# Edge messages of a graph layer: the attribute product written by ScalarE, the gathered rows added to it by the DMA, in three tile buffers

## The chip, the cores and the metric

The kernel runs on one core of a Trainium2 chip. The core has five engines with instruction queues of their own: TensorE (PE, with weight loads shown apart as PEld), VectorE (DVE), ScalarE (ACT), GpSimd (POOL) and SyncE (SP). SP and POOL start the DMAs here. The metric is the device time of one launch in microseconds (us), lower is better; the kernel before took 2510.64 us (median of 3 runs, 2509.55 to 2512.31).

## What is computed

```python
xn = layernorm(x)                                    # (3125, 256) nodes
# graph branch: 100000 edges, sorted by dst, 3 attributes each
m   = concat([xn[src], edge_attr], axis=1)           # (100000, 259)
tmp = relu(m @ W1.T + b1)                            # the message of an edge
h_N = segment_sum(tmp, dst, num_segments=3125)
g   = relu(concat([xn, h_N], axis=1) @ W2.T);  g = g / max(norm(g), 1e-12)
# mix branch: 4 layers on xn: linear attention (8 heads), then a GELU MLP 256 -> 1024 -> 256
x = x + g + mix(xn)
# then 16 experts, 2 per node, over layernorm(x), a second layernorm, and the sum with x
```

The message is split as `relu(P[src] + attr·A)`: `P = xn @ W1[:, :256].T` is made once for the 3125 nodes and kept in HBM as `P_d`, and the product of the three attributes and the bias is a small matmul for each tile of edges. This document is about how these two summands meet.

## The kernel before, in words

**Edge tiles.** The edges are cut into 224 tiles (`NPAIR`) of 500 edges that fall into one block of 125 destination nodes. A tile lies on 125 partitions, 4 edges on each (`ST = 4`); `k` counts its two halves of 2 edges (512 columns of f32). For tile p there is:

- SP brings the attributes, `aT` (`sp_attr`, L433), two tiles deep.
- PE makes the attribute product of both halves into the two PSUM banks `edge_bank` (L366).
- POOL starts four gathers (L758), each of 125 rows of 256 f32 from `P_d` into one of the slots of `G`. `G` has 8 slots, two tiles. The gathers of tile p+2 wait for `z_done` of tile p.
- DVE adds product and gathered rows into `z` (L406). That frees the PSUM banks and the slots of `G`.
- ACT takes `zr = relu(z)`, rounded to fp32r (L374); DVE takes the rest, `zl = relu(z) - zr` (L380).
- PE multiplies `zr` and `zl` by the one-hot matrix of destinations (L358, L359: 8 matmuls) into `sum_bank`, one tile late, and DVE adds that to `agg` (L386). DVE also makes the one-hot matrix of the next tile (L393).

**Where the tiles stand.** PE, ACT and DVE have instruction orders that are written out by hand. Four tiles come ahead of the mix layers (`EG_FIRST = 2` groups of 2), 216 stand between the matmuls of the 4 mix layers (54 in each), the last four behind them. A layer has two parts. The attention part (`first`, 5 groups of nodes) has two tiles for each group, close together: on ACT they stand on both sides of five copies into `es` (L885 and L888). The second part (`second`, 5 groups) has eight tiles for each group, `step(0)` to `step(7)`: step 0 ahead of the MLP's first matmul, steps 1 to 4 behind hidden pieces f = 0, 2, 4, 6 of W1, 5 behind the queries of the next group, 6 and 7 between the five output rows of W2. ACT evicts the hidden pieces (GELU, L914) out of a ring of three PSUM banks (`RING`), and PE can't write a bank until ACT has emptied it. POOL does nothing but gathers in all that time, in tile order.

Semaphores on this path: `at_in` (attributes have landed), `e_done` (product), `g_in` (a gather has landed, one for each slot), `z_done`, `r_done` (relu), `lo_done` (zl), `s_done` (sums), `acc_done`. After the edges come the graph output, the routing and the experts, which the change doesn't touch but for a name.

Of the kernel before, what the change touches and what calls it, by code (L numbers as in the profile page):

```python
# [11 lines left out]
def build(nc, x, src, dst, edge_attr, gnn_W1, gnn_b1, gnn_W2,  # L12
# [7 lines left out]
    N, D = x.shape  # L20
# [23 lines left out]
    PG = 2  # L44
    NEG = NPAIR // PG
    PQ = NPAIR // EC
# [8 lines left out]
    assert N == T * NT and E == SE * NS and NPAIR == PG * NEG == PQ * EC and MT % 4 == 0  # L55
# [12 lines left out]
    with ExitStack() as ctx:  # L68
# [12 lines left out]
        def sem(name):  # L81
# [112 lines left out]
        ATS = [part_rows(hn, 0), part_rows(hn, 600), part_rows(TT, 0), part_rows(TT, 600), part_rows(z, 0)]  # L194
# [94 lines left out]
        st_ready, e_done, z_done, r_done, lo_done, oh_done, s_done, acc_done = (sem(n) for n in (  # L289
            "st_ready", "e_done", "z_done", "r_done", "lo_done", "oh_done", "s_done", "acc_done"))  # L290
        g_in = [sem(f"g_in{i}") for i in range(PG * ST)]
# [57 lines left out]

        def pe_sums(ge, s):  # L350
# [3 lines left out]
            for i in range(ST):  # L354
                cols = slice(D * (i % 2), D * (i % 2) + D)
                if i % 2 == 0:
                    nc.tensor.wait_ge(lo_done, ge * 2 + (i // 2 + 3))
                nc.tensor.matmul(sum_bank[0:T, 0:D], onehot[:, s, i, :], zr[:, s, i // 2, cols], start=i == 0, stop=False)  # L358
                ins = nc.tensor.matmul(sum_bank[0:T, 0:D], onehot[:, s, i, :], zl[:, i // 2, cols], start=False, stop=i == ST - 1)  # L359
# [16 lines left out]
        def dve_low(ge, s):  # L376

            for k in range(2):
                nc.vector.wait_ge(r_done, ge * 2 + (k + 1))
                nc.vector.scalar_tensor_tensor(zl[:, k, :], z[:, k, :], 0.0, zr[:, s, k, :].bitcast(f32), ALU.max, ALU.subtract).then_inc(lo_done, 1)  # L380
# [16 lines left out]
        def dve_edges(e, ge, group, s, first=False, last=False):  # L397
# [3 lines left out]
            nc.vector.wait_ge(lo_done, ge * 2 + 2)  # L401
            for k in range(2):
                nc.vector.wait_ge(e_done, ge * 2 + (k + 1))
                for j in (ST * s + 2 * k, ST * s + 2 * k + 1):
                    nc.vector.wait_ge(g_in[j], group * 16 + 16)
                nc.vector.tensor_tensor(z[:, k, :], edge_bank[k][0:ET, :],  # L406
                                        G[:, ST * s + 2 * k:ST * s + 2 * k + 2, :].rearrange("p j d -> p (j d)"),
                                        ALU.add).then_inc(z_done, 1)
            if not first:
                dve_acc(ge - 1, reg)  # L410
            dve_low(ge, s)
            if not last:
                dve_onehot(e + 1, ge + 1, 1 - s)

        def pool_edges(r):

            def group(e, ge, s):
# [4 lines left out]
                for j in range(PG * ST):  # L422
                    if j % 2 == 0:
                        v = nc.gpsimd.snap(ge * (2 * PG) + (j // 2 + 1))
                        nc.gpsimd.wait_ge(z_done, v)
# [1314 lines left out]
```

## Time and profile before

| | |
|---|---|
| median of 3 runs | 2510.64 us |
| profiled execution, its time and span | 2507.48 us, 2505.6 us |
| PE busy (matmul) | 2054.5 us, 82% |
| DVE busy | 1571.3 us, 63% |
| ACT busy | 1032.5 us, 41% |
| POOL busy | 1317.4 us, 53% |
| mean granted TensorE clock | 0.917 |

The span by stages: to about 129 us the input, `P_d` and the edge tables; 129 to 148 us the first four tiles; then the four mix layers to about 1960 us; then graph output, routing and the experts. A line of the profile names the kernel's line, engine, operation and tiles. Idle time stands behind it with what ended it. Where POOL is between two DMA issues, "issue" means that it waited for nothing the profile shows. Idle time of an engine that nobody waits for costs nothing.

### The profile page before, as it was taken

How to read it: one execution, taken by the hardware profiler on the slowest of the kernel's cores; microseconds unless marked ns; L12 is line 12 of the kernel's file. 1: busy time of each engine (PE TensorE's matmuls, PEld its weight loads, DVE VectorE, ACT ScalarE, POOL GpSimd, SP SyncE). 2: the span in 40 equal slices, each digit the busy share in tenths (PEclk: the TensorE clock that was granted, in tenths of full speed). 3: DMA queues.
4: the chain of work that ended last, by engine and by line, in shares of the span. 5: the costliest groups of instructions: out<-in, count | busy, mean ns of one | idle time of the engine just before them, and what ended most of it. 6: DMA issues, size and time to landing. Idle time of an engine off the chain costs nothing. (4 is left out here: it accounts for less than half of the span.)

```text
span 2505.6 us, 37237 instructions
## 1 busy us (share of the span) xinstructions
PE 2054.5 (82%) x10686; PEld 1654.9 (66%) x10686; DVE 1571.3 (63%) x3709; ACT 1032.5 (41%) x2338; POOL 1317.4 (53%) x1112
## 2 busy tenths in 40 slices
PE   3368899998879999987999997889999773899920
PEld 2247677776757777766777776667777563799920
DVE  4667777766767777676777767777776557111126
ACT  1234544444434444444455544455544241333310
POOL 3164666666556666755666665566666300332255
PEclk9679999999989999998999999999999786899965
DMA  8632322224222222422222233222222331899943
GB/s 199 196 70 57 74 68 66 69 69 111 58 65 66 68 68 70 119 57 67 71 69 69 68 71 102 57 71 67 68 67 71 82 84 31 294 331 329 324 124 96
DMA packets 262791, 260.81 MB, mean 104 GB/s; under 512 B 150233, under 2 KB 195158, under 8 KB 262674
## 3 DMA queue, kind: packets, MB, share of 16 engines
q0 software_dynamic: 124672, 132.82, 21.7%
q1 hardware_dynamic: 133890, 126.67, 16.5%
q10 hardware_dynamic: 4112, 0.03, 0.1%
q8 instruction: 39, 0.64, 0.1%
q14 instruction: 78, 0.64, 0.1%
HBM read 229.85 MB, written 28.39 MB: 103 GB/s over the span
## 5 line engine op out<-in xcount | busy, mean ns | idle before, releaser
L758 POOL DMA_INDIRECT G<-P_d,src_T x896 | 1152.7, 1287 | 771.2 <-DVE z L406 484.1
L374 ACT ACTIVATE zr<-z 125x512 fp32r<-125x512 f32 x448 | 274.3, 638 | 456.1 <-DVE z L406 309.8
L406 DVE TENSOR_TENSOR z<-bank,G 125x512 f32<-125x512 f32 x448 | 291.9, 686 | 231.9 <-PE bank L366 101.0
L1169 PE MATMUL bank<-TT,W_s 128*128 128x250 f32 (+1 forms) x1280 | 374.2, 444 | 5.0 <-ACT TT L827 4.2
L1040 PE MATMUL bank<-W_s,hid 128*125 128x256 f32 x1600 | 359.5, 379 | 0.0
L1040 PEld LDWEIGHTS bank<-W_s,hid 128*125 128x125 f32 x1600 | 292.6, 187 | 42.8
L1169 PEld LDWEIGHTS bank<-TT,W_s 128*128 128x128 f32 x1280 | 243.8, 197 | 110.5 <-ACT TT L827 14.2
L380 DVE SCALAR_TENSOR_TENSOR zl<-z,zr 125x512 fp32r<-125x512 f32 x448 | 288.1, 684 | 39.8 <-ACT zr L374 22.1
L358 PE MATMUL bank<-zr,onehot 125*125 125x256 f32 x896 | 270.9, 334 | 7.5 <-DVE zl L380 7.2
L1034 PE MATMUL bank<-ident,hn 125*128 125x125 f32 x700 | 136.2, 305 | 117.8 <-DVE hn L1377 50.0
L359 PE MATMUL bank<-zl,onehot 125*125 125x256 f32 x896 | 229.7, 287 | 0.0
L827 ACT ACTIVATE TT<-bank,lnc 128x125 f32<-128x125 f32 x600 | 214.3, 475 | 32.3 <-PE bank L1034 29.7
L914 ACT ACTIVATE hid<-bank,b1c 128x375 f32<-128x375 f32 x320 | 164.7, 521 | 106.1 <-PE bank L1169 90.7
L358 PEld LDWEIGHTS bank<-zr,onehot 125*125 125x125 f32 x896 | 172.9, 193 | 32.6 <-issue 12.0
L1034 PEld LDWEIGHTS bank<-ident,hn 125*128 125x128 f32 x700 | 79.5, 148 | 173.1 <-ACT TT L827 56.0
L366 PE MATMUL bank<-Wst,aT 128*125 128x512 bf16 x448 | 141.7, 397 | 54.3 <-DMA aT<-attr_d 43.0
L359 PEld LDWEIGHTS bank<-zl,onehot 125*125 125x125 f32 x896 | 173.5, 194 | 5.5
L1518 DVE TENSOR_TENSOR X<-bank,X 125x256 f32<-125x256 f32 x200 | 84.8, 424 | 121.0 <-PE bank L1040 120.7
L772 POOL DMA_INDIRECT xs<-zn_d,slot_tok x32 | 30.3, 948 | 239.0 <-DVE slot_tok L1689 164.9
L393 DVE TENSOR_TENSOR onehot<-iota_n,dst_T 125x500 fp32r<-125x500 f32 x224 | 151.6, 677 | 0.0
L1040 PE MATMUL bank<-Wv_s,TT 128*125 128x256 f32 x400 | 100.4, 390 | 29.5 <-DVE V L1445 29.5
L1040 PE MATMUL bank<-Wq_s,TT 128*125 128x256 f32 x400 | 105.1, 405 | 16.9 <-DVE qe L1472 13.1
(282 smaller groups left out, 3029.5 us busy)
## 6 DMA issues: line engine op xcount, KB each, us to landing
W_s<-in_L_ffn_w SPq DMA_DIRECT2D x64, 512.0 KB
hid<-in_L_ffn_w SPq DMA_DIRECT2D x64, 512.0 KB
G<-P_d,src_T POOLq DMA_INDIRECT x896
W_s<-in_L_mix_W SPq DMA_DIRECT2D x8, 1024.0 KB
aT<-attr_d SPq DMA_DIRECT2D x224, 31.2 KB
slot_out<-yo SPq DMA_DIRECT2D x32, 128.0 KB
slot_out<-eT SPq DMA_DIRECT2D x32, 128.0 KB
attr_d<-hn SPq DMA_DIRECT2D x12, 246.1 KB, 4.0
```

The source lines that it names most:

```text
L358: nc.tensor.matmul(sum_bank[0:T, 0:D], onehot[:, s, i, :], zr[:, s, i // 2, cols], start=i == 0, stop=False)
L359: ins = nc.tensor.matmul(sum_bank[0:T, 0:D], onehot[:, s, i, :], zl[:, i // 2, cols], start=False, stop=i == ST - 1)
L374: nc.scalar.activation(zr[:, s, k, :], z[:, k, :], ACT.Relu).then_inc(r_done, 1)
L380: nc.vector.scalar_tensor_tensor(zl[:, k, :], z[:, k, :], 0.0, zr[:, s, k, :].bitcast(f32), ALU.max, ALU.subtract).then_inc(lo_done, 1)
L393: nc.vector.tensor_tensor(onehot[:, s, :, :], iota_n[0:ET, :].unsqueeze(1).to_broadcast([ET, ST, T]), dst_T[:, ds(e * ST, ST)].unsqueeze(2 ...
L406: nc.vector.tensor_tensor(z[:, k, :], edge_bank[k][0:ET, :], G[:, ST * s + 2 * k:ST * s + 2 * k + 2, :].rearrange("p j d -> p (j d)"), ALU ...
L758: pool.indirect_dma_start(G[:, j, :], None, P_d[:, :], bass.IndirectOffsetOnAxis(ap=src_T[:, at:at + 1], axis=0)).then_inc(g_in[j], 16)
L827: ins = act.activation(TT[:, k, tt_cols(j)], RING[loc % 3][:, 128 * k:128 * k + T], ACT.Identity, bias=shift(k), scale=gain(k))
L914: act.activation(hid[:, f, a * T:b * T], RING[loc % 3][:, 0:(b - a) * T], ACT.Gelu, bias=b1c[:, f:f + 1]).then_inc(ring_act, 1)
L1034: ins = pe.transpose(to[:, 128 * k:128 * k + parts], rows[:, 128 * k:128 * k + 128], ident[0:parts, 0:parts])
L1040: ins = pe.matmul(to[0:parts, 0:cols], a, b, start=i == 0, stop=i == len(products) - 1)
L1169: ins = pe.matmul(to[:, 0:(b - a) * T], W1_s[:, k, part], TT[:, k, TT_PIECES[pc]], start=k == 0, stop=k == KD - 1)
```

## The change

It does the following, and nothing outside of the edges changes but line numbers and the name of one scratch area (`z` becomes `G` in `ATS`):

- The sum z by DVE and the tile `z` are gone. ACT copies the product out of `edge_bank` into the tile's slots of `G` (`act_attr`), and the gathers are issued with `compute_op=ALU.add`: they add the rows of `P_d` to what stands in `G`.
- `G` has 12 slots, three tiles (`GS = 3`). `zl` has two buffers.
- ACT reads `G` for relu (`act_relu`) and waits there for `g_in`; behind it stands the copy for the tile after next. DVE's `dve_low` reads `G`.
- PE's product for tile p+2 stands where that of tile p stood.
- A gather of tile p+2 waits for `v_done`, the copy of the product of tile p+2.

```diff
+    GS = 3
-        G = sb("G", [ET, PG * ST, D])
-        z = sb("z", [ET, 2, 2 * D])
-        zl = sb("zl", [ET, 2, 2 * D], f32r)
+        G = sb("G", [ET, GS * ST, D])
+        zl = sb("zl", [ET, PG, 2, 2 * D], f32r)
+        def pe_products(ge, group, s):
+            nc.tensor.wait_ge(at_in[s], group * 16 + 16)
+            for k in range(2):
+                nc.tensor.wait_ge(v_done, ge * 2 + (k + 1))
+                nc.tensor.matmul(edge_bank[k][0:ET, :], aT[:, s, :], Wst[:, 2 * k * D:2 * (k + 1) * D],
+                                 start=True, stop=True).then_inc(e_done, 1)
...
-        def pe_edges(ge, group, s, first=False):
-            nc.tensor.wait_ge(at_in[s], group * 16 + 16)
-            for k in range(2):
-                nc.tensor.wait_ge(z_done, ge * 2 + (k + 3))
-                nc.tensor.matmul(edge_bank[k][0:ET, :], aT[:, s, :], Wst[:, 2 * k * D:2 * (k + 1) * D],
-                                 start=True, stop=True).then_inc(e_done, 1)
+        def pe_edges(ge, group, s, first=False, last=False):
+
+            if not last:
+                pe_products(ge + PG, group + 1, s)
             if not first:
                 pe_sums(ge - 1, 1 - s)
-        def act_edges(ge, s):
+        def act_attr(ge, q, gap=GS):
             for k in range(2):
-                nc.scalar.wait_ge(z_done, ge * 2 + (k + 5))
-                nc.scalar.activation(zr[:, s, k, :], z[:, k, :], ACT.Relu).then_inc(r_done, 1)
+                nc.scalar.wait_ge(e_done, ge * 2 + (k + 1))
+                nc.scalar.wait_ge(lo_done, ge * 2 + (k + 1 + 2 * (GS - gap)))
+                nc.scalar.activation(messages(q, k), edge_bank[k][0:ET, :], ACT.Copy).then_inc(v_done, 1)
+
+        def act_relu(ge, q, s, arrived):
+            nc.scalar.wait_ge(s_done, ge + 1)
+            for k in range(2):
+                for j in (ST * q + 2 * k, ST * q + 2 * k + 1):
+                    nc.scalar.wait_ge(g_in[j], arrived * 16)
+                nc.scalar.activation(zr[:, s, k, :], messages(q, k), ACT.Relu).then_inc(r_done, 1)
...
-        def dve_edges(e, ge, group, s, first=False, last=False):
+        def dve_edges(e, ge, q, s, first=False, last=False):
             reg = None if first else block_of(e - 1)
             if first:
                 dve_onehot(e, ge, s)
-            nc.vector.wait_ge(lo_done, ge * 2 + 2)
-            for k in range(2):
-                nc.vector.wait_ge(e_done, ge * 2 + (k + 1))
-                for j in (ST * s + 2 * k, ST * s + 2 * k + 1):
-                    nc.vector.wait_ge(g_in[j], group * 16 + 16)
-                nc.vector.tensor_tensor(z[:, k, :], edge_bank[k][0:ET, :],
-                                        G[:, ST * s + 2 * k:ST * s + 2 * k + 2, :].rearrange("p j d -> p (j d)"),
-                                        ALU.add).then_inc(z_done, 1)
+            dve_low(ge, q, s)
             if not first:
                 dve_acc(ge - 1, reg)
-            dve_low(ge, s)
             if not last:
                 dve_onehot(e + 1, ge + 1, 1 - s)
+
+        def pool_gather(at, q, i):
+            nc.gpsimd.indirect_dma_start(G[:, ST * q + i, :], None, P_d[:, :],
+                                         bass.IndirectOffsetOnAxis(ap=at, axis=0), compute_op=ALU.add).then_inc(g_in[ST * q + i], 16)
...
-                    if j % 2 == 0:
-                        pool.wait_ge(z_done, e * (2 * PG) + j // 2 + 1)
...
+            for p in range(NPAIR):
+                for i in range(ST):
+                    if i % 2 == 0:
+                        pool.wait_ge(v_done, p * 2 + (i // 2 + 3))
+                    pool_gather(src_T[:, p * ST + i:p * ST + i + 1], p % GS, i)
...
+                act_relu(p, p % GS, s, p // GS + 1)
+                if p + PG < NPAIR:
+                    act_attr(p + PG, (p + PG) % GS)
```

How the instructions stand now. On ACT, in the attention part, around the copies into `es` (they empty PE's transposes of `eT`), before:

```order
L374 ACTIVATE zr<-z 125x512 [waits z_done] x2
L833 ACTIVATE es<-bank 125x256 [waits ring_full] x5
L374 ACTIVATE zr<-z 125x512 [waits z_done] x2
L880 ACTIVATE corr<-cdiff 128x2 [waits cd_done]
L882 ACTIVATE eT<-bank,nb 128x375 x2
```

and now:

```order
L392 ACTIVATE zr<-G 125x512 [waits g_in9,g_in8,s_done]
L392 ACTIVATE zr<-G 125x512 [waits g_in11,g_in10]
L385 ACTIVATE G<-bank 125x512 [waits lo_done,e_done] x2
L843 ACTIVATE es<-bank 125x256 [waits ring_full] x5
L392 ACTIVATE zr<-G 125x512 [waits g_in1,g_in0,s_done]
L392 ACTIVATE zr<-G 125x512 [waits g_in3,g_in2]
L385 ACTIVATE G<-bank 125x512 [waits lo_done,e_done] x2
L895 ACTIVATE corr<-cdiff 128x2 [waits cd_done]
```

Two copies have come between the two relus, and each pair of relus waits for DMAs (`g_in`) where it waited for DVE.

On ACT, in the second part of a layer, around the hidden pieces of the MLP (`hid` is evicted out of the ring that PE writes), before:

```order
L914 ACTIVATE hid<-bank,b1c 128x375 [waits ring_full]
L914 ACTIVATE hid<-bank,b1c 128x250 [waits ring_full]
L374 ACTIVATE zr<-z 125x512 [waits z_done] x2
L914 ACTIVATE hid<-bank,b1c 128x375 [waits ring_full]
L914 ACTIVATE hid<-bank,b1c 128x250 [waits ring_full]
```

and now:

```order
L929 ACTIVATE hid<-bank,b1c 128x375 [waits ring_full]
L929 ACTIVATE hid<-bank,b1c 128x250 [waits ring_full]
L392 ACTIVATE zr<-G 125x512 [waits g_in5,g_in4,s_done]
L392 ACTIVATE zr<-G 125x512 [waits g_in7,g_in6]
L385 ACTIVATE G<-bank 125x512 [waits lo_done,e_done] x2
L929 ACTIVATE hid<-bank,b1c 128x375 [waits ring_full]
L929 ACTIVATE hid<-bank,b1c 128x250 [waits ring_full]
```

The evictions of `hid` now stand behind the landing of gathered rows and behind two copies.

## Rows read from the trace of the kernel before

**Rows 1.** Busy time of a stretch of layers, counts in brackets, clock, DMA share.
```profile
core 0: us, PE busy (x) PEld busy (x) DVE busy (x) ACT busy (x) POOL busy (x), PEclk, DMA share, GB/s
770.00:1170.00 400.00, 364.78 (x1856) 289.88 (x1856) 288.48 (x662) 187.29 (x400) 246.98 (x192) 0.98 0.30 73
```

**Rows 2.** PE's waits in 405 to 1950 us: total us, times, longest.
```profile
PE bank L1040 <- DVE V L1445: 21.8, 15, 3.2
PE bank L1034 <- DVE hn L1525: 20.5, 18, 1.2
PE bank L1034 <- DVE hn L1377: 14.1, 3, 4.8
PE bank L1107 <- ACT es L833: 12.4, 15, 0.8
PE bank L1040 <- DVE qe L1472: 10.3, 5, 3.4
PE bank L1034 <- DVE qe L1480: 8.5, 3, 2.8
...
PE bank L358 <- DVE zl L380: 3.4, 6, 0.8
```

**Rows 3.** The page's costliest groups: busy, mean ns, idle before, what ended it.
```profile
L758 POOL DMA_INDIRECT G<-P_d,src_T x896 | 1152.7, 1287 | 771.2 <-DVE z L406 484.1
L374 ACT ACTIVATE zr<-z 125x512 fp32r<-125x512 f32 x448 | 274.3, 638 | 456.1 <-DVE z L406 309.8
L406 DVE TENSOR_TENSOR z<-bank,G 125x512 f32<-125x512 f32 x448 | 291.9, 686 | 231.9 <-PE bank L366 101.0
```

**Rows 4.** POOL in order of time, 806 to 856 us: start, us, idle before.
```profile
809.28 1.21 POOL L758 DMA_INDIRECT G<-P_d,src_T  x1 [11.63 <-DVE z L406]
...
826.51 1.35 POOL L758 DMA_INDIRECT G<-P_d,src_T  x1 [0.31 <-issue]
...
839.02 1.21 POOL L758 DMA_INDIRECT G<-P_d,src_T  x1 [0.31 <-issue]
```

**Rows 5.** DVE in order of time, same stretch: first and fifth tile's sums.
```profile
808.31 1.28 DVE L406 TENSOR_TENSOR z<-bank,G 125x512 f32<-125x512 f32 x2
...
830.87 0.69 DVE L406 TENSOR_TENSOR z<-bank,G 125x512 f32<-125x512 f32 x1 [0.66 <-DMA G<-P_d,src_T]
```

**Rows 6.** ACT in order of time, one group of the second part.
```profile
811.04 1.19 ACT L374 ACTIVATE zr<-z 125x512 fp32r<-125x512 f32 x2
...
819.41 1.23 ACT L374 ACTIVATE zr<-z 125x512 fp32r<-125x512 f32 x2 [0.85 <-DVE z L406]
...
822.82 0.57 ACT L914 ACTIVATE hid<-bank,b1c 128x375 f32<-128x375 f32 x1 [0.79 <-issue]
...
824.66 1.23 ACT L374 ACTIVATE zr<-z 125x512 fp32r<-125x512 f32 x2 [0.52 <-issue]
...
830.24 0.63 ACT L374 ACTIVATE zr<-z 125x512 fp32r<-125x512 f32 x1 [0.53 <-DVE z L406]
...
842.22 1.23 ACT L374 ACTIVATE zr<-z 125x512 fp32r<-125x512 f32 x2 [5.52 <-DVE z L406]
...
874.78 1.20 ACT L374 ACTIVATE zr<-z 125x512 fp32r<-125x512 f32 x2
```

**Rows 7.** POOL and DVE in order of time, around the first four tiles.
```profile
88.99 1.24 POOL L758 DMA_INDIRECT G<-P_d,src_T  x1 [42.83 <-issue]
...
129.18 1.29 DVE L406 TENSOR_TENSOR z<-bank,G 125x512 f32<-125x512 f32 x2 [15.45 <-PE bank L366]
...
145.87 0.69 DVE L406 TENSOR_TENSOR z<-bank,G 125x512 f32<-125x512 f32 x1 [2.83 <-DMA G<-P_d,src_T]
```

**Rows 8.** ACT in order of time, two tiles of the attention part.
```profile
1098.41 1.19 ACT L374 ACTIVATE zr<-z 125x512 fp32r<-125x512 f32 x2
1099.44 1.66 ACT L833 ACTIVATE es<-bank 125x256 f32<-125x256 f32 x5
1101.72 1.23 ACT L374 ACTIVATE zr<-z 125x512 fp32r<-125x512 f32 x2 [0.61 <-DVE z L406]
```

**Rows 9.** Two lines of indirect DMAs on POOL: ns min/median/max, first and last start.
```profile
L758 POOL DMA_INDIRECT G<-P_d,src_T x768: 1205/1211/2137, 379.2 to 1968.8; - x192
...
L772 POOL DMA_INDIRECT xs<-zn_d,slot_tok x32: 944/944/969, 2134.9 to 2365.1; - x32
```

More of the change, by code:

```diff
@@ L54, in build @@
     MT = (2 * N + NE * (SL - 1)) // SL
[L55 removed]
+    assert N == T * NT and E == SE * NS and NPAIR == PG * NEG == PQ * EC and MT % 4 == 0 and NPAIR % GS == PG
     def dram(name, shape, dt):
@@ L287, in build @@
         a_out = [sem(f"a_out{i}") for i in range(AB)]
[L289 to L291 removed]
+        st_ready, e_done, v_done, r_done, lo_done, oh_done, s_done, acc_done = (sem(n) for n in (
+            "st_ready", "e_done", "v_done", "r_done", "lo_done", "oh_done", "s_done", "acc_done"))
+        g_in = [sem(f"g_in{i}") for i in range(GS * ST)]
         at_in = [sem(f"at_in{i}") for i in range(PG)]
@@ L629, in layer @@
                     weights_A(l + 1)
-                with sp.Fori(EG_B + 1, EG_L + 1) as g:
+                with sp.Fori(EG_B + 2, EG_L + (1 if last else 2)) as g:
                     e = l * EG_L + g + EG_FIRST
@@ L854, in both @@
                     edges(group, s)
+            for p in range(PG):
+                act_attr(p, p)
             for e in range(EG_FIRST):
@@ L929, in _, with again, act_first @@
                 both(e)
-            more_rounds(act, act_tables, lambda r: both(r * NEG), lambda e, ge: both(ge), lambda r: both(r * NEG + (NEG - 1)))
+            def again(ge, last=False):
+                for s in range(PG):
+                    act_relu(ge * PG + s, s, s, ge + GATHERS)
+                    if not last:
+                        act_attr(ge * PG + (s + PG), s, gap=PG)
+            def act_first(r):
+                for s in range(PG):
+                    act_attr(r * NPAIR + s, s, gap=PG)
+                again(r * NEG)
+            more_rounds(act, act_tables, act_first, lambda e, ge: again(ge), lambda r: again(r * NEG + (NEG - 1), last=True))
             def rows_T(u):
@@ L1061, in _, with edges, both @@
             pe.wait_ge(t_cp, 5)
-            def edges(group, s, first=False):
-                pe_edges(group * PG + s, group, s, first=first)
-            def both(group, first=False):
+            def edges(group, s, first=False, last=False):
+                pe_edges(group * PG + s, group, s, first=first, last=last)
+            def both(group, first=False, last=False):
+                if first:
+                    for s in range(PG):
+                        pe_products(group * PG + s, group, s)
                 for s in range(PG):
-                    edges(group, s, first=first and s == 0)
+                    edges(group, s, first=first and s == 0, last=last)
             for e in range(EG_FIRST):
@@ L1185, in _ @@
                 second(NG - 1, last=True)
-            with pe.Fori(EG_LAST, NEG) as e:
-                both(e)
+            for e in range(EG_LAST, NEG):
+                both(e, last=e == NEG - 1)
             pe_sums(NPAIR - 1, 1)
@@ L1195, in pe_last @@
             def pe_last(r):
-                both(r * NEG + (NEG - 1))
+                both(r * NEG + (NEG - 1), last=True)
                 pe_sums(r * NPAIR + (NPAIR - 1), 1)
@@ L1395, in edges @@
             def edges(e, group, s, first=False, last=False):
-                dve_edges(e * PG + s, group * PG + s, group, s, first=first, last=last)
+                dve_edges(e * PG + s, group * PG + s, (e * PG + s) % GS if isinstance(group, int) else s, s, first=first, last=last)
             def both(e, group, first=False, last=False):
```

38 lines of the change are left out of this document (17 added, 21 removed).

## The prediction

> **What bounds the kernel now.** I read the busy time by stages first, then who waits for whom, then the order of time on POOL, DVE and ACT over one group of nodes. In the mix layers PE is busy 364.78 of 400 us at a clock of 0.98 [rows 1]. So the layers, where 216 of the 224 tiles stand, are PE's, and DVE (288), POOL (247) and ACT (187) have room on average. PE's idle time there that DVE ends is 21.8 + 20.5 + 14.1 + 10.3 + 8.5 + 3.4 = 78.6 us [rows 2]; that bounds what a relieved DVE can give back. POOL has the least obvious schedule. It idles 771 us, but 484 of that waits for the sum z [rows 3], and then it works in bursts: from 809.28 us it issues 20 gathers without a pause, the last at 839.02 [rows 4], so (839.02 + 1.21 + 0.30 - 809.28) / 5 = 6.25 us for a tile of four. PE's steps in that stretch are closer: relus start at 819.41 and 824.66 [rows 6]. The burst is survived by a head start. Its last tile but one is just caught: the gather that starts at 826.51 is issued until 827.86, and z runs at 830.87, released by that DMA [rows 4, 5]. From the end of an issue to the landing it is therefore 3.0 us.
>
> **What the change removes.** DVE loses 448 sums of 686 ns, 292 us busy [rows 3]. Most of it is cover that PE never waited for. The waits in front of L1445 and L1525 end on work that stands ahead of the tile steps or in a chain of its own, so of the 78.6 us I take 10, with 0 and 78.6 as the ends.
>
> **What it adds on ACT.** 448 copies of 125x512. The nearest row is the relu of the same size, 638 ns, two in 1.23 us [rows 3, 6]; the end above is 0.75 us each, and nothing below 0.6 is to be expected from the same 512 columns. It is 286 us more on an engine at 187 of 400. In the MLP they cost nothing by themselves: behind two hidden pieces ACT has an idle 0.79 us before one eviction [rows 6] and the wait in front of relu, and PE's ring of three banks covers the order. In the attention part they are exposed. There PE waits for the copies into `es` [rows 2], and the second relu follows the first by 1101.72 - 1098.41 = 3.31 us, of which relu and copies take 2.7 [rows 8]. With two attribute copies between them it is 1.23 + 1.23 + 1.66 + about 0.1 = 4.2 us, 0.9 more, 20 groups: **+18 us**.
>
> **What it moves: the start of the gathers.** Three buffers sound like a deeper queue. They are not: the copy for tile p+2 stands behind relu of tile p on ACT, and only then may POOL start on p+2. Two tiles are outstanding, as before, and the third buffer only holds the tile that is being read. Worse, the start moves from DVE's sum to ACT's step.
>
> - MLP bursts. POOL's burst starts at 809.28, after z at 808.31 [rows 4, 5]. ACT's step 0 comes behind ten evictions at 811.04 [rows 6]; two relus (1.23) and the first copy (0.64) put the burst's start at 812.9, 3.6 us later. At 6.25 us for a tile and 3.0 us to land (issue gap of 0.3 not counted), the second halves of the next tiles are there at 821.9, 828.1 and 834.4. The relus of these halves start at 820.0 (819.41 + 0.6), 825.3 and 830.9 [rows 6]. The lateness is 1.9, 2.8 and 3.5 us. The fourth, 840.6, is in time for 842.22 + 0.6. While ACT waits for rows, the evictions behind it wait, and PE runs out of banks after 0.8 us of slack. So 3.5 - 0.8 = 2.7 us in each group, 20 groups: **+54 us**. The period of a group, 874.78 - 811.04 = 63.7 us, becomes that much longer.
> - Tail of a group (steps 5 to 7) and end of a layer. PE's product at step p waited for z(p-1); it now waits for the copy for tile p+1, which stands behind relu(p-1), the same landing and 1.23 us more. 20 groups: **+25 us**.
> - First four tiles. POOL fetches two tiles at 88.99, long before the first z at 129.18, and the fourth tile's last sum runs at 145.87 [rows 7]. In the changed kernel no gather can start before the first product has been copied, about 130 us. Sixteen gathers in series take 25 us, landing 3: the last relu comes at 158 us for 146.6 now: **+11 us**.
>
> Sum with gathers that cost what they cost now: 18 + 54 + 25 + 11 - 10 = +98 us.
>
> **What the accumulating gather costs.** No row shows one. It does all that a plain gather does and reads the destination besides, so it is not cheaper. The ends: 1.21 us as now, and 2.13, the longest gather [rows 9]; landing between 3.0 us and twice that, 6.0. The row nearest in kind is the pair of rows 9: the same instruction with nearly as many rows of the same size takes 944 ns into one place and 1211 ns into another, so the layout of its descriptors is worth 0.27 us. An addition must fetch the destination too. I take half of that step, 1.35 us, and 1 us more to land. A tile then costs POOL 6.8 us for 6.25. At the third tile of a burst that is 3 x 0.55 + 1.0 = 2.6 us later, 20 groups, 53 us. In the tail the landing alone counts, 1.0 x 20 = 20 us. The start gets 16 x 0.14 + 1 = 3 us. Together **+76 us**.
>
> Two pages of the Trainium skill speak against this change. "DMA: Bandwidth & Descriptors" (Rules for kernel authors) says that an accumulating DMA reads its destination before it writes it, and "Collectives: The Full Stack" (The bandwidth ceiling) that a DMA that adds runs at half the rate since it needs two reads, not because the addition costs anything. The first page (Why a DMA increments its semaphore by 16) also says that the number of engines is the largest divisor up to 16 of the slowest dimension: 5 for 125 rows. At its 27 GiB/s for an engine, 25 rows of 1 KB are an estimated 0.9 us, so a second read would put the landing at 3.9 us. The trace shows only the 3.0 us as a whole; by that estimate the sum stays where it is, by a rate that isn't changed it would be 20 to 40 us less.
>
> **Sum.** The profiled execution takes 2507.5 us (span 2505.6), 3 below the median of the runs, 2510.6. 2507.5 + 98 + 76 = 2681.5; I forecast **2680 us**. A measurement of this kernel tells 0.2%, 5 us, from no change.
>
> **Rivals.**
>
> 1. *The addition is free on POOL and in the transfer.* The first sum stands alone: 2507.5 + 98 = 2605 us. For it: POOL's median doesn't move with anything in 768 gathers [rows 9]. Against: a second read of each row. Chance 0.26.
> 2. *POOL becomes the bound of the layers.* Eight tiles must be issued in a group's 63.7 us, that is 1.99 us for a gather with its gap of 0.31. From 1.68 us on, POOL sets the period outright, and from 1.55 on it is late at the end of a group as well. At 1.8 us: 8 x 4 x 2.11 = 67.5 us plus the start and the landing that nothing covers (about 5 us), 9 us more in each of 20 groups, 180, beside 18 + 11 + 25 and the pairs of the attention part (4 x 0.6 us in 20 groups, 48): about 2790 us. At the upper end of 2.13 us it is near 2900. For it: POOL is already the engine with the longest unbroken work. Against: the step from 1.21 is large. Chance 0.20.
> 3. *Faster: DVE's relief is worth more than the lateness.* DVE is the engine that ends most of PE's idle time [rows 2]. If the relu waits under 0.8 us at the third tile of a burst, so that the ring hides it, only 18 + 11 remain against up to 78.6: at best 2507.5 + 29 - 78.6 = 2458 us, and with half of the relief 2497. The lateness of 3.5 us would have to be wrong by 2.7, for instance by ACT's step 0 coming two microseconds earlier. Chance 0.07.
> 4. *No difference.* Lateness and relief cancel, within 5 us of 2510. Chance 0.04.
>
> **How the numbers follow.** The forecast has 0.43 and its own range 2630 to 2750; rivals 1 to 4 have 0.26, 0.20, 0.07 and 0.04. Slower by over 0.2% has 0.89, no change 0.04, faster 0.07. For the range I leave out faster and same (0.11) and the upper half of rival 2, and take rival 1 with 25 us below it: 2580 to 2860.
>
> **What would show it.** The gather's line on POOL with its median: 1.21 for rival 1, 1.3 to 1.5 for the forecast, 1.7 or more for rival 2. ACT's relu should wait for `DMA G` in total for some hundreds of us, where DVE waited; PE's idle time in the second part should stand ahead of W1 products and be ended by ACT; POOL's idle time should shrink from 771 us; the first relu pair of a burst should be in time and the third late. The first four tiles should end some 11 to 15 us later. I am wrong if relu hardly waits for DMAs, or if POOL's burst starts earlier than ACT's step 0 lets it.

## The result and the profile after

The changed kernel takes 2902.62 us (median of 4 runs, 2901.37 to 2903.93), the kernel before 2511.47 us (median of 4, 2509.55 to 2512.36) on the same chip: ratio 1.156, 95% interval 1.154 to 1.158. It is 391 us slower, where I forecast 170 slower and gave a range that ended at 2860. The direction held and the size did not; what happened is nearest to rival 2, POOL as the bound of the layers' second part.

The first view is the page's list of costliest groups of the changed kernel (busy us, mean ns of one, idle us before, what ended it), which answers to [rows 3]:

```profile
L427 POOL DMA_INDIRECT G<-P_d,src_T x896 | 1827.4, 2039 | 489.8 <-issue 248.9
L399 DVE SCALAR_TENSOR_TENSOR zl<-G,zr 125x512 fp32r<-125x512 f32 x448 | 303.2, 693 | 935.2 <-ACT zr L392 911.6
L392 ACT ACTIVATE zr<-G 125x512 fp32r<-125x512 f32 x448 | 277.7, 641 | 740.2 <-DMA G<-P_d,src_T 739.5
L1198 PE MATMUL bank<-TT,W_s 128*128 128x250 f32 (+1 forms) x1280 | 412.7, 471 | 127.5 <-ACT hid L929 120.9
...
L385 ACT ACTIVATE G<-bank 125x512 f32<-125x512 f32 x448 | 242.2, 598 | 44.9 <-issue 36.1
```

The gather's mean went from 1287 to 2039 ns, 675 us more on POOL. The relu now waits 739.5 us for gathers, and DVE sits idle behind relu. The copy itself is cheap, 598 ns. POOL's idle time is 489.8 us, of which 248.9 is only the gap between two issues (`issue`). The view of POOL's operations on `G` gives the median, to be set beside [rows 9] (ns as minimum/median/maximum), and then what POOL's idle time ended on (us, times):

```profile
L427 POOL DMA_INDIRECT G<-P_d,src_T x896: 1986/1992/2849, 124.6 to 2361.1; - x180
...
  ACT G L385: 241.0, 82
```

The median is 1992 ns where it was 1211. Of the 771 us that POOL had to spare, 241 are left as real waits, in 82 pieces. In order of time, POOL around one MLP group (start, us, idle before), which answers to [rows 4]:

```profile
952.11 1.99 POOL L427 DMA_INDIRECT G<-P_d,src_T  x1 [5.31 <-ACT G L385]
954.41 1.99 POOL L427 DMA_INDIRECT G<-P_d,src_T  x1 [0.31 <-issue]
...
1025.14 1.99 POOL L427 DMA_INDIRECT G<-P_d,src_T  x1 [0.31 <-issue]
1030.85 2.01 POOL L427 DMA_INDIRECT G<-P_d,src_T  x1 [3.71 <-ACT G L385]
```

Between 952.11 and 1027.13 stand 32 gathers without a pause, all eight tiles of a group; before, the burst was 20 gathers long. A group lasts 1030.85 - 952.11 = 78.7 us. Of that, 75.0 are POOL's own time (32 x 2.30 = 73.6 at the median, and four gathers that took 2.4 to 2.5 us), and 3.7 us are a wait for the next copy. Most groups took 63.7 to 66.4 us before. Over all 20 groups POOL waits for 97 us of 1561 in pauses of over 0.4 us; in the kernel before it was 233 of 1245. ACT in order of time in the same group, beside [rows 6]:

```profile
950.13 1.20 ACT L392 ACTIVATE zr<-G 125x512 fp32r<-125x512 f32 x2
951.17 1.13 ACT L385 ACTIVATE G<-bank 125x512 f32<-125x512 f32 x2
...
960.74 0.63 ACT L392 ACTIVATE zr<-G 125x512 fp32r<-125x512 f32 x1 [1.79 <-DMA G<-P_d,src_T]
965.27 0.63 ACT L392 ACTIVATE zr<-G 125x512 fp32r<-125x512 f32 x1 [3.90 <-DMA G<-P_d,src_T]
...
975.11 0.63 ACT L392 ACTIVATE zr<-G 125x512 fp32r<-125x512 f32 x1 [4.65 <-DMA G<-P_d,src_T]
...
983.54 0.63 ACT L392 ACTIVATE zr<-G 125x512 fp32r<-125x512 f32 x1 [4.05 <-DMA G<-P_d,src_T]
```

The relus come two and two no longer, and the second half of each tile waits about 4 us for its rows. The gather that starts at 954.41 is issued until 956.40 and its relu runs at 960.74: 4.3 us to the waiting engine, where [rows 4, 5] had 3.0. Over all relus that a gather released, the median from the end of the issue is 4.4 us; over the sums z of the kernel before it is 3.1. Who pays is in the list of PE's waits from 400 to 2300 us (total us, times, longest), beside [rows 2]:

```profile
PE bank L1198 <- ACT hid L929: 115.4, 38, 4.8
PE bank L1060 <- ACT hid L929: 54.2, 15, 5.0
```

PE waits for the evictions that stand behind a waiting relu, as the prediction said; before, no such row was in the list. A stretch of 400 us in the same layer, which begins three tiles later than that of [rows 1]:

```profile
945.00:1345.00 400.00, 329.33 (x1514) 253.05 (x1515) 191.42 (x455) 194.18 (x420) 327.71 (x161) 0.91 0.48 63
```

POOL has gone from 247 to 328 busy of 400; with a gap of 0.31 us behind each of 161 gathers that is 378, nearly full. PE does 1514 matmuls where it did 1856. The share of DMA time is 0.48 where it was 0.30, at fewer GB/s. The page's row of POOL's DMA queue (packets, MB, share of 16 engines) has what goes with it, first of before, then of after:

```profile
q0 software_dynamic: 124672, 132.82, 21.7%
```

```profile
q0 software_dynamic: 382720, 133.81, 36.1%
```

Nearly the same bytes go in three times as many packets: 258048 more, 288 for each of 896 gathers.

### The profile page after: what moved, and what is told of

Same layout as the page of the kernel before. It is cut to its first block and busy times, and to the rows that moved or that the text cites. A ratio compares the mean times of both kernels' runs of the same rounds, so it can differ in the third digit from the quotient of the medians.

```text
span 2901.7 us, 37993 instructions
## 1 busy us (share of the span) xinstructions
PE 2170.2 (75%) x10686; PEld 1720.6 (59%) x10686; DVE 1320.1 (45%) x3261; ACT 1227.8 (42%) x2786; POOL 1992.1 (69%) x1112
## 3 DMA queue, kind: packets, MB, share of 16 engines
q0 software_dynamic: 382720, 133.81, 36.1%
## 5 line engine op out<-in xcount | busy, mean ns | idle before, releaser
L427 POOL DMA_INDIRECT G<-P_d,src_T x896 | 1827.4, 2039 | 489.8 <-issue 248.9
L399 DVE SCALAR_TENSOR_TENSOR zl<-G,zr 125x512 fp32r<-125x512 f32 x448 | 303.2, 693 | 935.2 <-ACT zr L392 911.6
L392 ACT ACTIVATE zr<-G 125x512 fp32r<-125x512 f32 x448 | 277.7, 641 | 740.2 <-DMA G<-P_d,src_T 739.5
L1198 PE MATMUL bank<-TT,W_s 128*128 128x250 f32 (+1 forms) x1280 | 412.7, 471 | 127.5 <-ACT hid L929 120.9
L366 PE MATMUL bank<-zr,onehot 125*125 125x256 f32 x896 | 293.6, 355 | 17.9 <-DVE agg L405 15.4
L385 ACT ACTIVATE G<-bank 125x512 f32<-125x512 f32 x448 | 242.2, 598 | 44.9 <-issue 36.1
L367 PE MATMUL bank<-zl,onehot 125*125 125x256 f32 x896 | 247.7, 303 | 0.0
L1060 PEld LDWEIGHTS bank<-ident,hn 125*128 125x128 f32 x700 | 82.0, 153 | 240.0 <-ACT hid L929 63.7
L366 PEld LDWEIGHTS bank<-zr,onehot 125*125 125x125 f32 x896 | 189.3, 211 | 44.1 <-issue 30.2
L355 PEld LDWEIGHTS bank<-Wst,aT 128*125 128x125 bf16 x448 | 64.7, 150 | 151.2 <-issue 82.5
L1066 PE MATMUL bank<-Wq_s,TT 128*125 128x256 f32 x400 | 125.8, 472 | 31.1 <-DVE qe L1501 29.2
L1066 PEld LDWEIGHTS bank<-Wq_s,TT 128*125 128x125 f32 x400 | 90.9, 242 | 61.4 <-DVE qe L1501 43.2
```

The source lines that it names most:

```text
L385: nc.scalar.activation(messages(q, k), edge_bank[k][0:ET, :], ACT.Copy).then_inc(v_done, 1)
L392: nc.scalar.activation(zr[:, s, k, :], messages(q, k), ACT.Relu).then_inc(r_done, 1)
L399: nc.vector.scalar_tensor_tensor(zl[:, s, k, :], messages(q, k), 0.0, zr[:, s, k, :].bitcast(f32), ALU.max, ALU.subtract).then_inc(lo_done, 1)
L427: nc.gpsimd.indirect_dma_start(G[:, ST * q + i, :], None, P_d[:, :], bass.IndirectOffsetOnAxis(ap=at, axis=0), compute_op=ALU.add).then_in ...
L1060: ins = pe.transpose(to[:, 128 * k:128 * k + parts], rows[:, 128 * k:128 * k + 128], ident[0:parts, 0:parts])
L1066: ins = pe.matmul(to[0:parts, 0:cols], a, b, start=i == 0, stop=i == len(products) - 1)
```

## Experiments

Three theories were to be told apart: that POOL's time for an adding gather makes the loss, on top of a smaller one from the order of work (theory T), that the order of work makes it (S), and that the DMA traffic makes it (D). The table has the time of three parts of the edge work, read from the starts of the relus in ACT's order of time: from the launch to the relu of the fourth tile, the first 14 tiles of each of the four layers (attention part), their other 40 tiles (MLP part, 20 groups), and what is left of the span. "Tile" is POOL's time for four gathers with all that stands between them, at the median. A time in the table is of the profiled execution, a ratio of the runs on one chip; "plain" is a gather without the addition (in the changed kernel the rows of `P_d` then overwrite the attribute product), "filler" a memset on POOL of that many us behind each gather.

| kernel | ratio (95%) | tile | start | attention | MLP | rest |
|---|---|---|---|---|---|---|
| before | 1 | 6.1 | 143.1 | 558.0 | 1245.0 | 559.5 |
| after | 1.156 (1.154 to 1.158) | 9.2 | 161.2 | 598.4 | 1561.1 | 581.0 |
| before, adding | 1.129 (1.125 to 1.133) | 9.2 | 159.6 | 593.5 | 1497.0 | 575.4 |
| after, plain | 1.032 (1.028 to 1.035) | 6.1 | 148.6 | 558.3 | 1311.3 | 571.2 |
| after, copy first | 1.149 (1.145 to 1.152) | 9.2 | 159.3 | 618.4 | 1528.0 | 583.3 |
| after, plain, copy first | 1.021 (1.020 to 1.023) | 6.1 | 149.8 | 567.3 | 1277.7 | 562.5 |
| after, 128 rows | 1.075 (1.071 to 1.078) | 7.4 | 152.2 | 576.6 | 1389.3 | 572.1 |
| after, plain, filler 0.80 | 1.144 (1.142 to 1.147) | 8.8 | 157.2 | 648.8 | 1491.9 | 579.8 |
| after, plain, filler 0.42 | 1.082 (1.080 to 1.083) | 7.3 | 153.1 | 594.7 | 1389.8 | 568.5 |
| after, plain, copy first, 128 rows | 1.003 (1.002 to 1.005) | 5.0 | 145.1 | 551.5 | 1261.4 | 555.4 |
| before, 128 rows | 0.990 (0.989 to 0.992) | 5.0 | 137.6 | 540.7 | 1242.0 | 555.5 |
| before, three deep | 0.996 (0.994 to 0.997) | 6.1 | 142.0 | 554.0 | 1241.0 | 554.1 |
| before, three deep, 128 rows | 0.988 (0.987 to 0.990) | 5.0 | 136.9 | 541.5 | 1242.0 | 553.8 |

### The change cut in two: the order without the addition, the addition without the order

```diff
 # after, plain: the gather of the changed kernel
-bass.IndirectOffsetOnAxis(ap=at, axis=0), compute_op=ALU.add)
+bass.IndirectOffsetOnAxis(ap=at, axis=0))
 # before, adding: the gather of the kernel before, and G cleared once
-bass.IndirectOffsetOnAxis(ap=src_T[:, at:at + 1], axis=0))
+bass.IndirectOffsetOnAxis(ap=src_T[:, at:at + 1], axis=0), compute_op=ALU.add)
```

> The changed kernel with plain gathers (no addition): the rows of P_d overwrite the attribute product, so the product is left out of the messages; order, waits and buffers stay. Theory T (the 391 us are POOL's time for an adding gather, 1.99 us for 1.21, on top of a schedule that costs about 100 us by itself): the gather is back at 1.21 us, landing 3.0 to 3.2 us, the kernel takes 2600 to 2625 us, a group of the second part 66 to 67 us. Theory S (the schedule costs most of it: ACT's evictions behind the rows, copies ahead of them): above 2750 us although the gather takes 1.21 us. Theory D (the additional DMA traffic slows the others): 2510 to 2540 us, since the traffic is gone.

> The kernel before with adding gathers and nothing else: G is cleared once and each gather adds to what stands there, so the message is wrong by the older rows in G; DVE still makes z. Theory T: the gather takes 1.99 us with a gap of 0.3 and lands after 4.0 us; eight tiles need 73.6 us where a group takes 63.7, so the second part follows POOL: 2760 to 2820 us. Theory S: the order is that of before, with DVE in front of ACT, so no more than 2560 us. Theory D: in between, with longer plain DMAs (weights, attributes) in the trace.

The order alone takes 2590.67 us (2585.78 to 2594.38), the addition alone 2832.71 (2827.81 to 2837.38), for 2512.45 of the kernel before. That is +78 and +320; the sum, 398, is the whole loss of 391 within the runs' spread. So the addition's cost is there without any of ScalarE's copies or the third buffer, which rules out theory S for most of the loss. The order alone came out 9 us below the range that I gave for it, though a full group takes 67 to 69 us where I expected 66 to 67. The gather of each, first the order alone (ns minimum/median/maximum):

```profile
L427 POOL DMA_INDIRECT G<-P_d,src_T x896: 1206/1214/2457, 124.4 to 2050.0; - x180
```

```profile
L759 POOL DMA_INDIRECT G<-P_d,src_T x896: 1982/1992/3055, 89.7 to 2287.5; - x180
```

The median follows the addition, and neither the order nor the third buffer. With the addition alone, the page's group of DVE's sum shows the wait that relu has in the changed kernel (columns as above):

```profile
L406 DVE TENSOR_TENSOR z<-bank,G 125x512 f32<-125x512 f32 x448 | 301.2, 688 | 590.7 <-DMA G<-P_d,src_T 471.1
```

The 320 us are above what I expected of it. Its MLP groups last 75.2 to 76.7 us (the last of each layer is shorter), and POOL pauses for no more than 1.5 us in any of them, where the changed kernel's pauses come to some 5. So in this kernel POOL's own time is the period of a group.

### ScalarE's copy ahead of the relu

```diff
-                act_relu(p, p % GS, s, p // GS + 1)
                 if p + PG < NPAIR:
                     act_attr(p + PG, (p + PG) % GS)
+                act_relu(p, p % GS, s, p // GS + 1)
```

> The changed kernel with ACT's copy for tile p+2 ahead of relu of tile p: the gathers start about 1.2 us earlier after each step and no longer behind the landing of tile p. Theory T: POOL is the bound of the second part and doesn't care for the order: 2885 to 2903 us, gather 1.99 us. Theory S: the order is what hurts, so at least 100 us come back: 2800 us or less.

> The changed kernel without the addition in the gathers (the attribute product is lost from G, so its output isn't the reference's), and with ScalarE's copies for tile p+2 placed ahead of the relu of tile p instead of behind it. It is compared with the same kernel with the copies behind the relu (2590.7 us), 78 us over the kernel before. If those 78 us are the late start of the bursts (two relus of 1.23 us ahead of the first copy, in the MLP groups and at the tails), the copies ahead give back up to 1.2 us in each of 20 groups at the third tile and as much in the tail: 2590 - 20 to 45 = 2545 to 2570 us. If the 78 us are ScalarE's added 286 us of copies themselves, wherever they stand, the time stays at 2590 within 6 us. If the pair in the attention part counts, its gap (3.57 us) shrinks toward 3.3.

With the addition 2884.3 us (2881.99 to 2890.88), 18 less than the changed kernel; without it 2559.07 us (2557.75 to 2564.98), beside 2507.24 of the kernel before on the same chip. The ratio falls from 1.032 to 1.021, some 27 us. All of it is in the MLP part (1311.3 to 1277.7) and the rest; the attention part gets 9 us longer. So about a third of the order's 78 us comes from the copy's place behind the relu; that it does so by the late start of the bursts fits the MLP part and isn't shown separately. With the addition the MLP part gains as much (1561.1 to 1528.0), but the attention part gives 20 of it back.

### Gathers of 128 rows in the changed kernel

```diff
-        src_T = sb("src_T", [ET, NPAIR * ST], i32)
+        src_T = sb("src_T", [128, NPAIR * ST], i32)
-        G = sb("G", [ET, GS * ST, D])
+        G = sb("G", [128, GS * ST, D])
```

> The changed kernel with gathers of 128 rows for 125 (G and the indices have 128 partitions, the last three rows aren't read). It asks what the 1.99 us consist of. If POOL's time goes by the rows that one DMA engine gets (the plain gather took 1.21 us with 125 rows, 0.94 with 128), the addition adds little: gather 1.15 to 1.3 us, landing 3.3 to 3.8 us, kernel 2600 to 2660 us. If POOL pays 0.78 us for about 125 additions whatever their place: gather 1.7 us, kernel 2790 to 2840 us. If nothing changes (1.99 us): 2900 us.

2696.66 us (2691.93 to 2699.97): three more rows in each gather make the kernel 206 us faster. The gather, and the queue:

```profile
L427 POOL DMA_INDIRECT G<-P_d,src_T x896: 1532/1541/2727, 123.7 to 2153.7; - x180
...
q0 software_dynamic: 139008, 134.59, 34.2%
```

The median falls between the two that I had named, 1.2 and 1.7. The packets fall from 382720 to 139008, but the share of DMA time stays at 34.2% (36.1 with 125 rows). Of a shorter span that is 12% less DMA time, 920 us for 1048, so this run alone doesn't clear the traffic; the filler of the next section does, with plain transfers. Packets of this queue and POOL's median have the same order in the four kinds, but no common price: plain 128 rows 52992 and 946 ns, plain 125 rows 124672 and 1211, adding 128 rows 139008 and 1541, adding 125 rows 382720 and 1992. Between the second and the third, 14336 packets more go with 330 ns more; between the third and the fourth, 243712 with 451. What in the addition holds POOL stays open.

### A filler on POOL in place of the addition

```diff
                     pool_gather(src_T[:, p * ST + i:p * ST + i + 1], p % GS, i)
+                    pool.wait_ge(padded, p * ST + i)
+                    pool.memset(pad[:, :], 0.0).then_inc(padded, 1)
```

`pad` has 820 columns of bf16 in the one kernel and 360 in the other; the gathers are plain.

> The changed kernel without the addition (the attribute product is lost from G, so its output isn't the reference's), with a memset of a scratch tile of some 0.8 us on POOL behind each of the 896 gathers. POOL's time for a gather with what follows it is then about that of the adding gather (1.99 + 0.31 us), while the transfer and its landing stay plain (2.8 us). If POOL's occupation is what the addition costs, the group of eight tiles comes to 8 x 4 x 2.3 = 74 us plus 3 to 5, and the time to 2820 to 2880 us, within 30 to 70 us of the changed kernel's 2902; the rest is the landing (1.1 us more, once a group and at each pair of the attention part). If the transfer is what costs (the reads of the destination, the single packets of a row, the later landing), the filler lies mostly beside it and the time stays under 2700 us.

> The same with half the filler, some 0.4 us behind each gather, so that gather, gap and filler make about 1.9 us. Eight tiles then take POOL 61 us, less than the 68 to 69 us that a group takes without a filler, but the bursts are later by 1.6 us a tile. If the group's period is the larger of POOL's sum and the schedule's with the burst's lateness on top (a knee), the time is 2650 to 2720 us, clearly less than half way from 2591 to the run with the full filler in slope only if the burst's lateness is small. If every us of POOL's time counts from the start (a straight line), half of the full filler's loss: 2700 to 2735 us. If POOL has room, 2591 to 2630 us.

2874.72 us (2867.27 to 2879.49) with the long filler, 2714.12 (2707.84 to 2715.57) with the short one. POOL in order of time with the long one:

```profile
901.45 1.22 POOL L429 DMA_INDIRECT G<-P_d,src_T  x1 [0.18 <-issue]
902.68 0.80 POOL L775 MEMSET pad<- 125x820 bf16 x1
903.66 1.22 POOL L429 DMA_INDIRECT G<-P_d,src_T  x1 [0.18 <-issue]
```

A plain gather and a memset take 2.21 us where the adding gather takes 2.30 with its gap, and the time is within 28 us of the changed kernel's with no addition anywhere: 284 of the 312 us between "after, plain" and "after" are back. The queue has the plain 124672 packets and 19.0% of DMA time, so theory D is ruled out for most of the loss. The page shows the same wait, though the transfers are the plain ones:

```profile
L394 ACT ACTIVATE zr<-G 125x512 fp32r<-125x512 f32 x448 | 274.7, 637 | 633.7 <-DMA G<-P_d,src_T 626.0
```

The three fillers, none, short and long, also give the shape of the curve. POOL's step is 1.52, 1.82 and 2.21 us at 2590.7, 2714.1 and 2874.7 us: 896 x 0.30 = 269 us more on POOL cost 123, and 896 x 0.39 = 349 more cost 161, both 0.46 us for each us. In the MLP part alone it is 0.41 for both. The ranges that I had given for a knee and for a straight line overlap at 2714 us, so it is the equal slopes that speak for a line. My knee stood at a gather of 1.55 to 1.68 us, which is a step of 1.86 to 1.99, between the two fillers; the fillers show none. The adding gathers bend a little: their steps of 1.52 (plain), 1.85 (128 rows) and 2.30 us have MLP parts of 1311.3, 1389.3 and 1561.1 us, 0.37 and then 0.59 us for each us of POOL. With a step of 1.82 a group lasts 71.6 us, 13 more than POOL's 58.2. With the long filler that distance has closed to 5.7 (76.4 for 70.7), near the 5.1 of the changed kernel (78.7 for 73.6). One pair needs no rate: the short filler and the adding gathers of 128 rows have nearly the same step, 1.82 and 1.85, and the same MLP part, 1389.8 and 1389.3 us, the one without and the other with the addition.

The filler isn't neutral. The long one is 50 us slower than the changed kernel in the attention part (648.8 for 598.4). DVE's own work is longer beside the memsets, in both parts: against "after, plain" its busy time grows by 55 us in the attention part and by 55 in the MLP part. As one example, the groups of one line that writes `hn` (times, total us, mean ns), 500 to 1800 us of "after, plain" and 500 to 2000 us of the long filler:

```profile
L1406 DVE TENSOR_SCALAR hn<-X,mvA,rstd_t 125x256 f32<-125x256 f32 x145 | 59.8, 476 | 0.0
```

```profile
L1410 DVE TENSOR_SCALAR hn<-X,mvA,rstd_t 125x256 f32<-125x256 f32 x140 | 103.1, 799 | 0.0
```

So the whole's 284 of 312 us says too much: part of it is DVE's slower work. PE's waits for `V`, made in the attention part, are 17.8 us in all with no filler, 65.5 with the long one and 30.2 in the changed kernel; its waits for `hn`, which grow in the MLP part above all, are 73, 100 and 85. The MLP part is the better comparison, though not a clean one. The addition costs 249.8 us there (1311.3 to 1561.1) and the filler 180.6. Its step is 0.09 us shorter than the adding gather's, which over 640 gathers is 58 us of POOL's time: 24 us at the rate of 0.41 that the fillers show, 58 if POOL is full. As an estimate, the time that POOL is held then accounts for 205 to 239 of 250 us. The rest, 11 to 45, is left for the later landing and all else, and up to some 28 us of the filler's own share may be DVE's.

### What the order is worth when POOL is relieved

This is the changed kernel without the addition, with the copy first and 128 rows.

> The changed kernel without the addition (same part left out), with the copy for tile p+2 ahead of the relu of tile p and with gathers of 128 rows: everything in the change's order that its loss on POOL and at the start of the bursts can be relieved of. Its DVE is still without the sum z. If the rest of the schedule's loss (52 us after the copies were moved) is waiting for gathers, a tile of 4 x 1.25 us on POOL takes most of it away: 2505 to 2525 us, and DVE's relief could show, below the old order with the same gathers (2481 us) only if it is worth more than all that is left. If the rest is ScalarE's own work in front of PE's evictions, 2545 to 2560 us.

2515.51 us (2513.87 to 2521.83), ratio 1.003, 0.3% slower than the kernel before and 1.3% slower than the old order with the same gathers. Here relu hardly waits for gathers any more (18.8 us in all), and ACT waits in front of its copies instead (page's groups):

```profile
L392 ACT ACTIVATE zr<-G 125x512 fp32r<-125x512 f32 x448 | 262.0, 648 | 18.8 <-DMA G<-P_d,src_T 18.8
...
L385 ACT ACTIVATE G<-bank 125x512 f32<-125x512 f32 x448 | 245.4, 607 | 255.5 <-PE bank L355 217.8
```

DVE does without the 292 us of sums here and the kernel is still behind. So the relief is worth less than what is left of the order's cost. That this is the copies on ACT isn't shown: of the 38 us between the two profiled spans 19 lie in the MLP part, 11 in the attention part and 8 at the start, and they weren't split by cause.

### Better gathers and a third buffer for the kernel before

```diff
 # before, three deep
-                    if j % 2 == 0:
-                        pool.wait_ge(z_done, e * (2 * PG) + j // 2 + 1)
+                    if i % 2 == 0 and p >= GS:
+                        pool.wait_ge(z_done, (p - GS) * 2 + (i // 2 + 5))
```

> The kernel before with gathers of 128 rows each (three rows more that nobody reads) instead of 125, nothing else changed. The theory that POOL's time for a gather has room in the kernel before (it idles 771 us, the burst's last tile but one is just in time): POOL's median falls from 1.21 to 0.94 to 0.97 us and the landing from 3.0 to about 2.2 us, and the time hardly moves, 2490 to 2510 us (0 to -20). The theory that the gathers of the kernel before set its period already at the bursts: 20 groups by up to 1 us more, 2480 us or less. If the layout does not matter for a plain gather in this place, the median stays 1.21 and so does the time.

> The kernel before, in which G is three tiles deep instead of two: the gathers for tile p+3 wait for the sum z of tile p, no attribute product by ScalarE, no addition in the DMA. It takes the change's third buffer alone. If depth is what the change wanted and the ScalarE step withheld it (the copy of tile p+2 behind relu p leaves two tiles outstanding), the bursts start a tile earlier and the time is 5 to 20 us below the kernel before, 2490 to 2507 us, and z's waits for the DMA fall from some 180 us. If the third buffer is worth nothing (the burst's lead was enough), 2507 to 2517 us.

> The kernel before with both: G three tiles deep and gathers of 128 rows. If POOL's gathers and their landings still end some of the idle time of the kernel before, the two add: 2485 to 2500 us. If either alone takes away all waits for gathers, it equals the better one of them.

128 rows: 2481.48 us (2477.82 to 2486.58). Three deep: 2495.24 (2493.13 to 2498.22). Both: 2477.3 (2474.27 to 2479.11), ratio 0.988 (0.987 to 0.990), the lowest median of this study, though not clear of 128 rows alone. The gather with 128 rows, and what waited for it (us, times):

```profile
L759 POOL DMA_INDIRECT G<-P_d,src_T x896: 940/946/1751, 88.9 to 1939.4; - x180
...
  DVE z L406: 9.9, 4
```

Of the 30 us between the spans of "before" and "before, 128 rows" 17 lie in the attention part and 6 at the start, and only 3 in the MLP part: its groups had hardly a wait to take away, as [rows 4, 5] said. I had expected at most 20 of the edit if POOL had room, and 27 or more if it had none; it gave 26. The two edits hardly add, since each takes away the same wait: z waits 9.9 us for gathers with the one and 3.8 with the other, where it waited 46.4 in the kernel before (not some 180, as I wrote for the third buffer).

## Why the prediction was wrong

- **What bounded the kernel before: right.** PE's layers, and bursts of gathers that were just in time. The loss is where I put most of it, 316 us of 396 between the profiled spans in the 20 MLP groups. One reading was short: the window of [rows 2] begins at 405 us and leaves out the attention part of the first layer. Over all four layers PE's waits for DVE are some 96 us, not 78.6, so rival 3 at its best was about 2441 us, not 2458.
- **The step that failed is "What the accumulating gather costs".** I took 1.35 us of POOL's time out of 1.21 to 2.13 and got 76 us from it. It measured 1.99, and 320 us in the old order, 312 in the new. Size was most of it, and form the rest: my sum let the third tile of a burst be late and no more. With 1.99 us and a landing 1.3 us later that formula gives 3 x 3.12 + 1.3 = 10.7 us in each of 20 groups, 26 in the tails and 14 at the start, about 2860 us in place of 2680. The remaining 43 us to 2903 are what a POOL that works through the whole group adds, or other parts' errors. The row that I leaned on, 944 and 1211 ns for two layouts [rows 9], is real: 128 for 125 rows gives 946 ns. But it is the price of another thing, and the addition has its own, 595 ns at 128 rows and 781 at 125. Half of the layout's step had no ground as an estimate for it. The upper half of the interval that I had from the longest gather deserved more than the 0.20 of rival 2. And its end was worked out too low: rival 2's own formula gives 32 x 2.44 + 5 - 63.7 = 19.4 us a group at 2.13 us, 388 in all, with 54 and 4 x 0.92 x 20 = 74 about 3020 us, not "near 2900", so the range that ended at 2860 left out more than I thought. The landing was nearly right: I took 4.0 us for 3.0, and it is 4.3 to the relu shown and 4.4 at the median, for 3.1. "DMA: Bandwidth & Descriptors" (Rules for kernel authors) of the Trainium skill says that such a DMA reads its destination before it writes it, and the later landing agrees with it; my estimate from that page was 3.9.
- **Rival 2 had the mechanism, and its formula is close in part by luck.** It said 32 gathers in a row and about 5 us that nothing covers for each group. Measured: 73.6 + 5.1 at the median, of which 3.7 are a pause. With 1.99 us in its formula, 73.6 + 5 - 63.7 = 15 us in each of 20 groups, 298, with 18 + 11 + 25 and 4 x 0.78 x 20 = 62 for the pairs, it gives 2507.5 + 414 = 2922 us; measured 2903. By parts that is 323 us for the MLP groups where 316 were measured, but 80 for the attention part where 40 were, 11 for the start where 18 were, and nothing for the 22 us behind the layers. Its threshold is not confirmed: there is loss below it, and the fillers' loss grows evenly from a step of 1.52 us on; the adding gathers cost more above it (0.59) than below (0.37), which one measured step on either side doesn't settle.
- **The first sum, +98 with gathers as cheap as before: 78 measured.** By parts:
  - *MLP bursts and tails, 54 + 25 = 79:* 66. The two were not separated. The copy ahead of the relu gives back 34 of them, which fits the mechanism that I named for both; for the other 32 it isn't shown.
  - *Attention pairs, +18, and DVE's relief, -10:* together 0.3. PE's wait for the copies into `es` did grow, from 12.4 [rows 2] to 27.0 us in three of the four layers; over the whole span, 20 waits each, from 16.5 to 36.0, 19.5 for the 18. The gap of a pair went only to 3.57 us, not 4.2. Against it stands PE's wait for DVE's `V`, over the whole span from 29.5 to 17.8, 12 less, where I had taken 10 for all of DVE. PE's waits of the kernel with the order alone, 400 to 2000 us:

```profile
PE bank L1136 <- ACT es L843: 27.0, 15, 1.8
...
PE bank L1066 <- DVE V L1474: 11.6, 15, 0.9
```

  - *First four tiles, +11:* 5.5 with plain gathers, 18 in the changed kernel for 14 predicted. POOL's first gather came at 124.4, not 130.
  - The rest, past the layers' parts, is 12 us longer, which I had no term for.
- **Rival 3** is ruled out by the kernel with the copy first, plain gathers and 128 rows: with hardly a wait for gathers left and DVE relieved, it takes 2516 us, and the old order with the same gathers 2481.
- **The signs** came true in kind: relu's wait for `DMA G`, PE's idle time ended by ACT ahead of W1 (115.4), POOL's idle time shrunk from 771 to 490 us. The gather's median, named first, pointed to rival 2.

## What to carry to other kernels

Price an operation that no row shows by what it occupies on its issuing engine, and put the chance where the engine's free time runs out: eight tiles of four gathers had 64 us, and the answer hung on one unknown of 0.8 us. An addition in an indirect DMA is not free for GpSimd, whatever it saves on DVE; compare that with the sum it removes (2 x 686 ns a tile on DVE against 4 x 781 ns on POOL). Look at the row count of a gather first: 128 rows for 125, three of them unread, made the kernel before 1% faster here, and the changed one 7%. A filler on the issuing engine tells the engine's time from the transfer's, but look at what it does to its neighbours before its whole effect is believed.

## What the hardware showed that I had not expected

- An adding gather holds POOL for longer than a plain one of the same bytes: 125 rows of 1 KB 1211 to 1992 ns, 128 rows 946 to 1541 ns, a factor of 1.63 to 1.65 in both.
- Fewer rows cost more: 125 rows take 1211 ns and 128 rows 946, with 124672 and 52992 packets in the queue for the same work, and the landing from the start of the issue has a median of 4.2 and 2.8 us (three deep, and 128 rows).
- A memset on POOL goes with longer times of some operations of DVE and leaves others alone: the `hn` of 125x256 went from 476 to 799 ns on average, while `zl` of 125x512 stayed at 690. By the page "SBUF — State Buffer" (Who interferes with whom) of the Trainium skill, DVE's `tensor_scalar` and `copy` can take the pair of ports that it shares with GpSimd, and whoever comes second is blocked for the whole instruction; an operation outside those modes with one input in SBUF does not contend. The trace agrees: beside `hn`, the `TENSOR_SCALAR` of `nb` went from 198 to 494 ns and the `COPY` of `mO` from 188 to 353, and the `TENSOR_TENSOR` of `agg` stayed at 417.
- Gathers go with the same. In the kernel before, the `COPY` of `mO` takes 170 ns on average with plain gathers of 128 rows, 246 with its own of 125, and 378 with adding ones of 125; that `hn` takes 405, 441 and 481 ns, less than the 754 that it takes over the whole span beside the long filler. What that is worth in time was not separated.
- PE's busy time rose with its idle time: 2054.5 us before, 2073.2 with the order alone, 2170.2 after, for the same 10686 matmuls, at a granted clock of 0.92, 0.92 and 0.88 over the span. PE is thus busy for 116 us more with the same matmuls, of 396 us between the profiled spans. The long filler shows the same (2168.2 us at 0.89), so it doesn't hang on the addition. How much of a group's longer period came by way of the clock was not separated.
